# Mask products behind the other sequence's exponent scores, and spline chunks two at a time

## The chip, the cores and the metric

The kernel runs on one core of one Trainium2 chip. The metric is device time in microseconds (us); lower is better. Its five engines each work through their own list of instructions in order and meet at semaphores: TensorE (PE) multiplies, VectorE (DVE) and ScalarE (ACT) empty its results out of PSUM, GpSimd (POOL) does leftovers, and SyncE (SP) issues the DMA transfers.

## The reference

A transformer layer on 16 sequences of 256 tokens, width 256, in float32:

```
x = x + attention(layernorm(x))      # 16 heads of 16; key j counts for query i only if j - i <= 16
x = x + ffn(layernorm(x))            # silu(x @ gate.T) * (x @ up.T) @ down.T, inner width 1024
```

The three weights of the second half are not given as matrices. Each is a cubic (Catmull-Rom) spline through some 2,030 control points, sampled at 262,144 places. The kernel builds them once, at its start.

## The kernel before

The sequences are taken two at a time in eight turns. What a turn does is cut into named steps, and the function `all_steps` (line 109) puts the steps of all turns into one list, sorted by a planned time for each; every engine walks this one list and does its own part of each step. So the table in `steps_of_turn` (line 95) sets the order on every engine, and a turn's attention lies among the second half of the turn before.

The steps that matter here, for each of two sequences (0 and 1) and eight pairs of heads (p), so n = 0 to 15:

- `s1` n: scores of two heads for the row maxima. PE does four products on 63 rows of the array, two in its upper half and two in its lower (line 616), and then two products over all 128 rows that add the mask (line 619): an identity times a triangle of -1e30, in bfloat16. DVE then takes the maxima, two reductions (line 510).
- `mt` s: the 16 heads' maxima of one sequence are turned over and stored by DMA as a 64th row beside the queries (`QM`).
- `sc` n: scores again, transposed, with the maxima taken off by that 64th row. PE does four products on 64 rows (line 636), ACT takes exp (line 418), and POOL cuts away what the mask forbids (lines 366 and 369).
- `av` n: values weighted, for four heads, on column quarters of the array (128*32 in the profile, line 644).
- `zt`, `ot`, `on`, `z2`: transposes. `qk`, `v`, `wo`: projections. `ga`, `up`, `ic`, `dn`: the second half; `ga` and `up` are six products of 512 columns each (lines 566 to 568), `dn`, `v` and `wo` twelve of 256 columns (lines 573 to 575). `x`, `xr`, `ld`, `y`: transfers. `la`, `lb`, `ma`, `mb`: layer norms.
- `ws` u: chunk u of 12 of the spline weights. PE makes two sums over 32 rows (line 589, four records in the trace), DVE joins them in two operations (lines 472 and 474), ACT and POOL split the result in two parts. Chunks 0 to 3 are gate, 4 to 7 up, 8 to 11 down.

`s1`, `sc` and `ws` share two buffers of two PSUM banks each (`pair0`, `pair1`), given in turns in the order of the list; a step on PE first waits until the step before it in its buffer has been emptied (`emptied`, line 244): for `s1` that is DVE's maxima, for `sc` ACT's exp, for `ws` DVE's sum. The other steps share four banks (`ring`). SP waits at each `ld` until `sc` of the turn before no longer reads what is overwritten.

Of the kernel before, what the change touches and what calls it, by code (L numbers as in the profile page):

```python
# [88 lines left out]

PERIOD = 62.0


def steps_of_turn():

    table = [("x", 0, 1, -70.2, 0), ("la", 0, 2, -62.2, 3.4), ("lb", 0, 2, -57.5, 2.25),
# [9 lines left out]
    return [(what, n + i, at + gap * i) for what, n, count, at, gap in table for i in range(count)]  # L107


def all_steps():  # L110

    out = [(t * PERIOD + at, what, t, n) for t in range(TURNS) for what, n, at in steps_of_turn()]
    out += [(-70, "raw", 0, 0), (-51, "split", 0, 0), (-47, "tap", 0, 0)]
    out += [((-33, -30.5, -28)[u] if u < 3 else -27 + 6.5 * (u - 2), "ws", 0, u) for u in range(CHUNKS)]
    return [i[1:] for i in sorted(out, key=lambda i: i[0])]


# [45 lines left out]
def build(nc, x, wqk, wv, wo, points, powers, rows, over, ident, identb, upper, out):  # L163
    ctx = ExitStack()
    with ctx:
# [78 lines left out]
        def emptied(step):  # L244
            what, t, n = step
            if what == "dn":
                return y_done, nth("y", t, n // 4)
            done = {"zt": zt_low, "qk": qk_low, "v": v_done, "mt": mt_done, "av": av_done, "ot": ot_done, "on": on_low,
                    "wo": wo_done, "z2": z2_low, "ga": ga_done, "up": up_done, "s1": max_done, "sc": exp_done,
                    "ws": ws_sum}[what]  # L250
            return done, nth(*step)

# [12 lines left out]
        def raw(i, n):  # L265
            return RAW[:, i * KB * D:(i + n) * KB * D].rearrange("p (k c) -> p k c", k=KB)

        def spline_part(u, part):
            m, j = divmod(u, 4)
            if m < 2:  # L270
                return (WGUh, WGUl)[part][:, m, j // 2, j % 2 * 512:(j % 2 + 1) * 512]
            return WD[:, 2 * j:2 * j + 2, part * D:(part + 1) * D]

        def spline_over(u):
            m, j = divmod(u, 4)
# [174 lines left out]
        def _(dve):  # L450
# [7 lines left out]
            for what, t, n in STEPS:  # L458
# [41 lines left out]
                elif what == "qk":  # L500
                    dve.wait_ge(qk_high, nth("qk", t, n))
                    low(STAGED[n][:, 1, :], bank(what, t, n)[:], STAGED[n][:, 0, :]).then_inc(qk_low, 1)
                elif what == "s1":
                    s, p = divmod(n, NP)
                    dve.wait_ge(s1_made, nth("s1", t, n))
                    if p == 0:
                        if t:
                            dve.wait_ge(mt_made, nth("mt", t - 1, s))
                    for it, cols in ((0, slice(0, W0)), (1, slice(W0, W0 + S))):
                        i = nc.vector.tensor_reduce(out=M[:, s, it, :].rearrange("p (a k) -> p a k", a=2)[:, :, p],  # L510
                                                    in_=pair(what, t, n)[:, :, cols], axis=AX.X, op=ALU.max, negate=True)
                    i.then_inc(max_done, 1)
                elif what == "mt":
                    dve.wait_ge(mt_made, nth("mt", t, n))
                    if t + n:
                        dve.wait_ge(m_loaded[1 - n], N_M * (t + n))
                    nc.vector.tensor_copy(MT[:], bank(what, t, n)[0:H, 0:S]).then_inc(mt_done, 1)
                elif what == "ot":
                    dve.wait_ge(ot_made, nth("ot", t, n))
                    if t:  # L520
                        dve.wait_ge(z2_made, nth("z2", t - 1, n // 2))
                    heads = bank(what, t, n)[:].rearrange("p (h c) -> p h c", c=2 * DH)
                    nc.vector.reciprocal(R[:, n, :], heads[:, :, DH]).then_inc(recip_done, 1)
                    dve.wait_ge(recip_done, nth("ot", t, n))
                    tt(Z[:, n, :].rearrange("p (h c) -> p h c", c=DH), heads[:, :, 0:DH],
                       R[:, n, :].unsqueeze(2).broadcast_to([128, H, DH]), ALU.mult).then_inc(ot_done, 1)
                elif what == "on":
                    dve.wait_ge(on_high, nth("on", t, n))
                    low(OTT[:, 1, :, :], halves(bank(what, t, n)), OTT[:, 0, :, :]).then_inc(on_low, 1)
                elif what == "wo":  # L530
                    dve.wait_ge(xr_loaded[t % 2][n], DMA * (t // 2 + 1))
                    dve.wait_ge(wo_made, nth("wo", t, n))
                    x1 = X1[t % 2][:, 2 * n:2 * n + 2, :]
                    tt(x1, x1, halves(bank(what, t, n)), ALU.add).then_inc(wo_done, 1)
                elif what == "z2":
                    dve.wait_ge(z2_high, nth("z2", t, n))
                    low(seq(YT, 1, n), halves(bank(what, t, n)), seq(YT, 0, n)).then_inc(z2_low, 1)
                elif what == "ga":
                    gu = GU[:, n % 2, :]
                    dve.wait_ge(tanh_done, nth("ga", t, n))  # L540
                    stt(out=gu, in0=gu, scalar=1.0, in1=bank(what, t, n)[:], op0=ALU.add, op1=ALU.mult).then_inc(ga_done, 1)  # L541
                elif what == "up":
                    gu = GU[:, n % 2, :]
                    dve.wait_ge(up_made, nth("up", t, n))
                    dve.wait_ge(ga_done, nth("ga", t, n))
                    tt(gu, gu, bank(what, t, n)[:], ALU.mult).then_inc(up_done, 1)  # L546
                elif what == "y":
                    dve.wait_ge(dn_made, nth("dn", t, 4 * n + 3))
                    x1 = X1[t % 2][:, 2 * n:2 * n + 2, :]
                    tt(x1, x1, halves(bank("dn", t, 4 * n)), ALU.add).then_inc(y_done, 1)  # L550

        @block.tensor
        def _(pe):
# [24 lines left out]
            for what, t, n in STEPS:  # L578
# [3 lines left out]
                    bk = bank(what, t, n)  # L582
                if what == "raw":
                    pe.wait_ge(ident_loaded, DMA)
                elif what == "ws":
                    pe.wait_ge(tapped, 1)
                    m, j = divmod(n, 4)
                    for part in range(2):
                        i = mm(pair(what, t, n)[:, part, :], ROWS[32 * m:32 * m + 32, part, :],  # L589
                               TAP[32 * m:32 * m + 32, j * 512:(j + 1) * 512], start=True, stop=True)  # L590
                    i.then_inc(ws_made, 1)
                elif what == "zt":
                    pe.wait_ge(norm_done[0], nth("lb", t, n))
                    turn_rows(bk, X, n, zt_made)
# [11 lines left out]
                elif what == "s1":  # L606
                    s, p = divmod(n, NP)
                    if p % HP == 0:
                        pe.wait_ge(qk_loaded[s][p // HP], N_QK * (t + 1))
                    if n == 0 and t == 0:  # L610
                        pe.wait_ge(mask_loaded, 2 * DMA)
                    pr = pair(what, t, n)
                    for it, c, w in ((0, 0, W0), (1, W0, S)):
                        for a in range(2):
                            r = slice(STACK * a, STACK * a + STACK - 1)
                            mm(pr[:, a, c:c + w], QM[r, s, p, it * 128:(it + 1) * 128], KS[r, s, p, 0:w],  # L616
                               start=it == 0, stop=False, skip_group_check=True)
                    for a in range(2):
                        i = mm(pr[:, a, AHEAD:AHEAD + 384].rearrange("p (i j) -> p i j", j=128)[:, 0:3:2, :],  # L619
                               IDB[:], UP[:].rearrange("p (i j) -> p i j", i=2), start=False, stop=True,  # L620
                               skip_group_check=True)
                    i.then_inc(s1_made, 1)
                elif what == "mt":
                    pe.wait_ge(max_done, nth("s1", t, n * NP + NP - 1))
# [97 lines left out]
```

## Time and profile before

| what | us |
|---|---|
| three runs, median (lowest to highest) | 720.44 (718.12 to 721.96) |
| profiled execution | 714.97 |
| its span, first to last instruction | 713.2 |
| PE busy in the span | 672.5 (94%) |
| DVE, ACT, POOL busy | 411.2, 263.6, 201.8 |
| mean granted clock of PE | 0.959 of full speed |

PE's matmuls are pipelined: the profile gives each a duration of its own that overlaps the next, so its cost is better read as the distance from its start to the next one's start. A row such as `L616 ... x4` merges neighbouring matmuls of one line. The granted clock has two levels, 1.00 (2.4 GHz) and 0.50 (1.2 GHz). Turns 2 to 6 look alike: from 163 us on, six stretches of 78 us follow each other and the first five differ by nothing that can be seen.

### The profile page before, as it was taken

What the parts mean: (1) busy time and instruction counts of PE and PEld (TensorE: products, weight loads), DVE (VectorE), ACT (ScalarE), POOL (GpSimd) and SP (SyncE); (2) the same over time, 40 slices, a digit from 0 to 9 for tenths busy, and PEclk for the clock granted to TensorE, in tenths of its full rate; (3) what the DMA queues carried; (4) which work ended last, traced back from release to release, by engine and by line L of the source; (5) the groups of instructions that cost most, each with busy time, mean ns of one, the idle gap of its engine ahead of it and who ended that gap; (6) DMA issues with size and microseconds to landing.
All of it is one profiled execution on the core that took longest, in us unless ns stands there. A gap on an engine that the chain in (4) does not pass through costs nothing.

```text
span 713.2 us, 12397 instructions
## 1 busy us (share of the span) xinstructions
PE 672.5 (94%) x4816; PEld 493.4 (69%) x4816; DVE 411.2 (58%) x828; ACT 263.6 (37%) x448; POOL 201.8 (28%) x244
## 2 busy tenths in 40 slices
PE   1799898999999999999999999999999999998997
PEld 0434554677687777877687768777787768776877
DVE  6556566665746475656656574657575563652540
ACT  1212333544433443443433444343433443343140
POOL 5023223213421333114321342124311341243040
PEclk9956697999999999999999999999999999999999
DMA  8221023112212221031201221131202111000000
GB/s 250 91 72 46 1 89 105 47 46 74 74 46 68 83 74 47 16 106 47 88 30 60 76 74 47 42 108 50 72 16 83 53 52 55 21 26 1 31 0 30
DMA packets 42873, 42.75 MB, mean 60 GB/s; under 512 B 4256, under 2 KB 42240, under 8 KB 42496
## 3 DMA queue, kind: packets, MB, share of 16 engines
q1 hardware_dynamic: 42816, 41.96, 17.7%
q8 instruction: 39, 0.64, 0.4%
q14 instruction: 18, 0.15, 0.1%
HBM read 12.32 MB, written 4.19 MB: 23 GB/s over the span
## 4 chain that ended last, share of the span: by engine, by line
PE 89%; DVE 5%; ACT 2%; issue 1%; POOL 1%; DMA 1%; POOLq 0%; ACTq 0%; DVEq 0%
PE ring L566 12%; PE ring L567 10%; PE ring L568 10%; PE ring L644 8%; PE ring L573 8%; PE pair L616 7%; PE ring L574 6%; PE ring L575 6%; PE pair L636 6%; PE pair L619 5%; PE pair L589 4%; PE ring L560 3%; PE ring L651 2%; ACT P L418 2%; DVE X L495 1%
## 5 line engine op out<-in xcount | busy, mean ns | idle before, releaser
L418 ACT ACTIVATE P<-pair 128x800 f32<-128x800 f32 x128 | 107.0, 838 | 133.0 <-PE pair L636 131.6
L510 DVE TENSOR_REDUCE M<-pair 128x2 f32<-128x288 f32 (+1 forms) x256 | 134.7, 569 | 25.8 <-PE pair L619 24.0
L374 POOL TENSOR_TENSOR IN<-GU,IN 128x512 fp32r<-128x512 f32 x64 | 82.3, 1286 | 145.5 <-ACT IN L379 145.5
L366 POOL TENSOR_SCALAR_AFFINE_SELECT P<-P 128x448 f32<-128x448 f32 x64 | 37.3, 582 | 250.3 <-ACT P L418 250.3
L566 PE MATMUL ring<-YT,WGUh 128*128 128x512 f32 x256 | 107.9, 421 | 0.1
L568 PE MATMUL ring<-YT,WGUl 128*128 128x512 f32 x256 | 101.6, 397 | 0.0
L567 PE MATMUL ring<-YT,WGUh 128*128 128x512 f32 x256 | 101.5, 396 | 0.0
L442 ACT ACTIVATE GU<-ring 128x512 f32<-128x512 f32 x64 | 38.3, 598 | 134.0 <-PE ring L568 134.0
L541 DVE SCALAR_TENSOR_TENSOR GU<-GU,ring 128x512 f32<-128x512 f32 x64 | 44.0, 688 | 72.8 <-ACT GU L442 72.8
L573 PE MATMUL ring<-WD,IN 128*128 128x256 f32 x256 | 77.9, 304 | 2.9 <-POOL IN L374 2.9
L616 PE MATMUL pair<-KS,QM 63*128 63x144 f32 (+1 forms) x512 | 67.4, 344 | 7.9 <-DVE M L510 3.2
L575 PE MATMUL ring<-WD,IN 128*128 128x256 f32 x256 | 73.5, 287 | 0.0
L574 PE MATMUL ring<-WD,IN 128*128 128x256 f32 x256 | 73.3, 286 | 0.0
L616 PEld LDWEIGHTS pair<-KS,QM 63*128 63x128 f32 x512 | 41.3, 200 | 43.2 <-issue 27.1
L644 PE MATMUL ring<-P,V 128*32 128x256 f32 (+1 forms) x1024 | 59.6, 352 | 3.3 <-POOL P L369 2.9
L636 PE MATMUL pair<-QM,KS 64*128 64x256 f32 (+1 forms) x512 | 58.4, 309 | 1.1 <-ACT P L418 0.9
L636 PEld LDWEIGHTS pair<-QM,KS 64*128 64x128 f32 x512 | 38.8, 189 | 29.0 <-issue 12.6
L566 PEld LDWEIGHTS ring<-YT,WGUh 128*128 128x128 f32 x256 | 48.2, 188 | 12.3 <-issue 0.5
L546 DVE TENSOR_TENSOR GU<-GU,ring 128x512 f32<-128x512 f32 x64 | 43.8, 685 | 21.8 <-PE ring L568 20.4
L568 PEld LDWEIGHTS ring<-YT,WGUl 128*128 128x128 f32 x256 | 48.2, 188 | 11.3
L567 PEld LDWEIGHTS ring<-YT,WGUh 128*128 128x128 f32 x256 | 48.5, 190 | 8.5
L573 PEld LDWEIGHTS ring<-WD,IN 128*128 128x128 f32 x256 | 49.5, 193 | 6.2 <-issue 4.9
(80 smaller groups left out, 1061.2 us busy)
## 6 DMA issues: line engine op xcount, KB each, us to landing
KS<-QKS SPq DMA_DIRECT2D x96, 128.0 KB, 2.1
QM<-X SPq DMA_DIRECT2D x48, 128.0 KB, 2.1
QM<-QKS SPq DMA_DIRECT2D x48, 128.0 KB, 2.1
X<-x SPq DMA_DIRECT2D x8, 512.0 KB, 3.9
X<-x SPq DMA_DIRECT2D x16, 256.0 KB, 2.9
out<-X SPq DMA_DIRECT2D x16, 256.0 KB, 2.2
OVER<-over SPq DMA_DIRECT2D x1, 1024.0 KB, 12.1
TAP<-points SPq DMA_DIRECT2D x1, 768.0 KB, 7.5
```

The source lines that it names most:

```text
L374: nc.gpsimd.tensor_tensor(IN[:, n, 1, :], GU[:, n % 2, :], IN[:, n, 0, :].bitcast(F32), ALU.subtract).then_inc(in_low, 1)
L418: nc.scalar.activation(P[:, g % 2, 2 * (n % 2):2 * (n % 2) + 2, :], pair(what, t, n)[:, :, 0:SW], ACT.Exp, scale=SCALE).then_inc(exp_done, 1)
L510: i = nc.vector.tensor_reduce(out=M[:, s, it, :].rearrange("p (a k) -> p a k", a=2)[:, :, p], in_=pair(what, t, n)[:, :, cols], axis=AX.X, ...
L566: mm(b[:], wh[:, kb], act[:, 0, kb, :], start=kb == 0, stop=False)
L567: mm(b[:], wh[:, kb], act[:, 1, kb, :], start=False, stop=False)
L568: i = mm(b[:], wl[:, kb], act[:, 0, kb, :], start=False, stop=kb == KB - 1)
L573: mm(b, act(k, 0), w[:, k, 0:D], start=first and k == 0, stop=False, skip_group_check=True)
L574: mm(b, act(k, 0), w[:, k, D:2 * D], start=False, stop=False, skip_group_check=True)
L575: i = mm(b, act(k, 1), w[:, k, 0:D], start=False, stop=False, skip_group_check=True)
L616: mm(pr[:, a, c:c + w], QM[r, s, p, it * 128:(it + 1) * 128], KS[r, s, p, 0:w], start=it == 0, stop=False, skip_group_check=True)
L636: i = mm(pr[:, a, c:c + w], KS[r, s, p, jt * 128:(jt + 1) * 128], QM[r, s, p, S - w:S], start=jt == 0, stop=jt == 1, skip_group_check=True)
L644: i = mm(bk[32 * hl:32 * hl + 32, S - w:S], V[:, n // NG * 2 + jt, n % NG * 4 + hl, :, :].rearrange("p a c -> p (a c)"), P[:, n % 2, hl, c ...
```

## The change

1. **Mask split off.** The two mask products of `s1` become a step `mk` of their own, and DVE's maxima wait for that step. `s1` keeps the four 63-row products.
2. **Beats.** A new table puts `s1` n, `sc` of the other sequence and `mk` n next to each other, sixteen times in a turn: `s1` 0 to 7 of the next turn with `sc` 8 to 15, and `s1` 8 to 15 with `sc` 0 to 7. The other steps are spread anew in between. As the two kinds alternate strictly, every `s1` now takes the same one of the two PSUM buffers and every `sc` the other.
3. **Couples.** Chunks are numbered so that 2k is a gate and 2k+1 an up chunk (rows 0 to 31 and 32 to 63 of the array), and for u below 8 PE does two chunks in one step, their matmuls alternating. Both PSUM buffers must be empty first. Chunks 8 to 11 stay single. `tap`, the operation that prepares their input, stands behind `qk` 2 on DVE, and six chunks stand ahead of the first `s1`.

```diff
+PERIOD = 65.96
+                  ("qk", 0, 4, 1, -59.74, 2.32), ("s1", 0, 8, 1, -31.77, 3.0),
+                  ("mk", 0, 8, 1, -31.73, 3.0), ("ld", 2, 2, 1, -26.2, 11.38),
...
+        def chunk(u):
+            return (u % 2, u // 2) if u < 8 else (2, u - 8)
...
-                elif what == "ws":
+                elif what == "ws" and (n % 2 or n >= 8):
                     pe.wait_ge(tapped, 1)
-                    m, j = divmod(n, 4)
+                    us = (n - 1, n) if n < 8 else (n,)
+                    if n < 8 and BEFORE.get((what, t, n - 1)):
+                        pe.wait_ge(*emptied(BEFORE[what, t, n - 1]))
                     for part in range(2):
-                        i = mm(pair(what, t, n)[:, part, :], ROWS[32 * m:32 * m + 32, part, :],
-                               TAP[32 * m:32 * m + 32, j * 512:(j + 1) * 512], start=True, stop=True)
-                    i.then_inc(ws_made, 1)
+                        for u in us:
+                            m, j = chunk(u)
+                            i = mm(pair(what, t, u)[:, part, :], ROWS[32 * m:32 * m + 32, part, :],
+                                   TAP[32 * m:32 * m + 32, j * 512:(j + 1) * 512], start=True, stop=True)
+                            if part:
+                                i.then_inc(ws_made, 1)
...
                 elif what == "s1":
...
                             mm(pr[:, a, c:c + w], QM[r, s, p, it * 128:(it + 1) * 128], KS[r, s, p, 0:w],
                                start=it == 0, stop=False, skip_group_check=True)
+                elif what == "mk":
+                    if n == 0 and t == 0:
+                        pe.wait_ge(mask_loaded, 2 * DMA)
+                    pr = pair("s1", t, n)
                     for a in range(2):
                         i = mm(pr[:, a, AHEAD:AHEAD + 384].rearrange("p (i j) -> p i j", j=128)[:, 0:3:2, :],
                                IDB[:], UP[:].rearrange("p (i j) -> p i j", i=2), start=False, stop=True,
                                skip_group_check=True)
                     i.then_inc(s1_made, 1)
```

PE in a turn of the middle, before: `sc` 6 (line 636), a step `qk`, and `s1` 14 with its mask (lines 616 and 619).

```order
L636 MATMUL pair0<-QM,KS 128x256 x2
L636 MATMUL pair0<-QM,KS 128x144 x2
L566 MATMUL ring0<-ZT,WQKh 128x512
L567 MATMUL ring0<-ZT,WQKh 128x512
L568 MATMUL ring0<-ZT,WQKl 128x512
L566 MATMUL ring0<-ZT,WQKh 128x512
L567 MATMUL ring0<-ZT,WQKh 128x512
L568 MATMUL ring0<-ZT,WQKl 128x512
L616 MATMUL pair1<-KS,QM 128x144 x2
L616 MATMUL pair1<-KS,QM 128x256 x2
L619 MATMUL pair1<-UP,IDB 128x2x128 x2
```

After, at the same place: a beat of `s1` 14 (L637), `sc` 6 (L661) and `mk` 14 (L644), and the step `up` 0 behind it.

```order
L637 MATMUL pair0<-KS,QM 128x144 x2
L637 MATMUL pair0<-KS,QM 128x256 x2
L661 MATMUL pair1<-QM,KS 128x256 x2
L661 MATMUL pair1<-QM,KS 128x144 x2
L644 MATMUL pair0<-UP,IDB 128x2x128 x2
L584 MATMUL ring0<-YT,WGUh 128x512
L585 MATMUL ring0<-YT,WGUh 128x512
L586 MATMUL ring0<-YT,WGUl 128x512
```

The 63- and 64-row products stand together now, and the full-array mask products moved behind both.

After, on PE: beats 4 and 5 of a turn (counted by the n of `s1`, from 0), with only one `av` (L669) between them, and the first `dn` (L591 to L593) behind.

```order
L637 MATMUL pair0<-KS,QM 128x144 x2
L637 MATMUL pair0<-KS,QM 128x256 x2
L661 MATMUL pair1<-QM,KS 128x256 x2
L661 MATMUL pair1<-QM,KS 128x144 x2
L644 MATMUL pair0<-UP,IDB 128x2x128 x2
L669 MATMUL ring1<-P,V 32x256 x4
L669 MATMUL ring1<-P,V 32x144 x4
L637 MATMUL pair0<-KS,QM 128x144 x2
L637 MATMUL pair0<-KS,QM 128x256 x2
L661 MATMUL pair1<-QM,KS 128x256 x2
L661 MATMUL pair1<-QM,KS 128x144 x2
L644 MATMUL pair0<-UP,IDB 128x2x128 x2
```

The second `s1` goes to the same `pair0` as the first, which DVE must have read by then.

At the start, after, PE has the chunks in couples (L611), the two buffers alternating; before it had two matmuls of one buffer, then two of the other.

```order
L611 MATMUL pair0<-TAP,ROWS 128x512
L611 MATMUL pair1<-TAP,ROWS 128x512
L611 MATMUL pair0<-TAP,ROWS 128x512
L611 MATMUL pair1<-TAP,ROWS 128x512
L611 MATMUL pair0<-TAP,ROWS 128x512
L611 MATMUL pair1<-TAP,ROWS 128x512
```

Six such rows are one and a half couples; three couples now come ahead of the first `s1`, where three single chunks came before.

## Rows read from the trace of the kernel before

**Rows 1.** The page: the chain that ended last, share of the span by engine.

```profile
PE 89%; DVE 5%; ACT 2%; issue 1%; POOL 1%; DMA 1%; POOLq 0%; ACTq 0%; DVEq 0%
```

**Rows 2.** Windows: from:to, length, busy us (count) per engine, clock, DMA share, GB/s.

```profile
30.00:115.00 85.00, 79.36 (x380) 40.96 (x379) 51.10 (x92) 23.28 (x41) 22.37 (x24) 0.74 0.19 63
...
163.00:241.00 78.00, 77.60 (x600) 58.83 (x601) 47.35 (x100) 31.70 (x55) 22.26 (x28) 1.00 0.19 62
...
631.00:713.00 82.00, 73.35 (x474) 61.63 (x472) 30.24 (x54) 22.42 (x39) 22.78 (x24) 0.96 0.04 14
```

**Rows 3.** Timeline of PE, turn 4: start, us, line, operation, tiles, shape, count.

```profile
330.49 0.50 PE L616 MATMUL pair<-KS,QM 63*128 63x144 f32 x4
330.92 0.39 PE L619 MATMUL pair<-UP,IDB 128*128 128x256 bf16 x2
331.07 0.47 PE L566 MATMUL ring<-YT,WGUh 128*128 128x512 f32 x1
331.38 0.40 PE L567 MATMUL ring<-YT,WGUh 128*128 128x512 f32 x1
331.62 0.40 PE L568 MATMUL ring<-YT,WGUl 128*128 128x512 f32 x1
...
335.31 0.28 PE L574 MATMUL ring<-WO,OTT 128*128 128x256 f32 x1
335.43 0.28 PE L575 MATMUL ring<-WO,OTT 128*128 128x256 f32 x1
335.64 0.45 PE L636 MATMUL pair<-QM,KS 64*128 64x256 f32 x4
336.02 0.50 PE L566 MATMUL ring<-YT,WGUh 128*128 128x512 f32 x1
336.36 0.40 PE L567 MATMUL ring<-YT,WGUh 128*128 128x512 f32 x1
```

**Rows 4.** Timeline of PE where `s1` directly follows `sc`, and the next.

```profile
346.88 0.45 PE L636 MATMUL pair<-QM,KS 64*128 64x256 f32 x4
347.17 0.43 PE L616 MATMUL pair<-KS,QM 63*128 63x144 f32 x4
347.54 0.39 PE L619 MATMUL pair<-UP,IDB 128*128 128x256 bf16 x2
348.26 0.50 PE L616 MATMUL pair<-KS,QM 63*128 63x144 f32 x4 [0.33 <-ACT P L418]
```

**Rows 5.** Timeline of DVE, ACT and POOL in the same stretch.

```profile
347.96 2.21 DVE L510 TENSOR_REDUCE M<-pair 128x2 f32<-128x288 f32 x4 [0.29 <-PE pair L619]
347.37 0.84 ACT L418 ACTIVATE P<-pair 128x800 f32<-128x800 f32 x1 [2.13 <-PE pair L636]
348.11 0.62 ACT L379 ACTIVATE IN<-GU 128x512 fp32r<-128x512 f32 x1
349.42 1.27 POOL L374 TENSOR_TENSOR IN<-GU,IN 128x512 fp32r<-128x512 f32 x1
```

**Rows 6.** Timeline of PE at the start.

```profile
30.14 6.49 PE L589 MATMUL pair<-TAP,ROWS 32*128 32x512 f32 x12
...
40.67 3.78 PE L589 MATMUL pair<-TAP,ROWS 32*128 32x512 f32 x4
...
65.36 0.69 PE L636 MATMUL pair<-QM,KS 64*128 64x256 f32 x8
...
106.75 0.50 PE L616 MATMUL pair<-KS,QM 63*128 63x144 f32 x4 [0.50 <-DVE W L474]
```

**Rows 7.** Timeline of DVE at the start.

```profile
21.50 2.28 DVE L466 TENSOR_TENSOR TAP<-TAP,POWER 96x2048 f32<-96x2048 f32 x1
...
44.49 0.69 DVE L472 TENSOR_TENSOR W<-pair,OVER 128x512 f32<-128x512 f32 x1 [2.65 <-PE pair L589]
```

**Rows 8.** Timeline of PE in the last turn.

```profile
650.90 0.89 PE L644 MATMUL ring<-P,V 128*32 128x256 f32 x16 [2.03 <-POOL P L369]
...
668.87 0.63 PE L560 MATMUL ring<-ID,Z 128*128 128x128 f32 x4 [0.46 <-DVE Z L495]
```

More of the change, by code:

```diff
@@ L87, in spline_tables, with steps, steps_of_start @@
             over.astype(np.float32))
-PERIOD = 62.0
-def steps_of_turn():
-    table = [("x", 0, 1, -70.2, 0), ("la", 0, 2, -62.2, 3.4), ("lb", 0, 2, -57.5, 2.25),
[9 rows of a table removed]
-    return [(what, n + i, at + gap * i) for what, n, count, at, gap in table for i in range(count)]
+PERIOD = 65.96
+def steps(table):
+    return [(what, n + by * i, at + gap * i) for what, n, count, by, at, gap in table for i in range(count)]
+def steps_of_start():
+    return steps([("raw", 0, 1, 1, -100.24, 0), ("split", 0, 1, 1, -63.32, 0), ("tap", 0, 1, 1, -54.24, 0),
+                  ("ws", 0, 4, 2, -45.21, 6.09), ("ws", 1, 4, 2, -45.18, 6.09),
+                  ("ws", 8, 4, 1, 24.16, 6.37)])
+def steps_of_turn():
+    return steps([("x", 0, 1, 1, -90.73, 0), ("la", 0, 2, 1, -73.48, 2.94), ("lb", 0, 2, 1, -69.39, 2.04),
[14 rows of a table added]
 def all_steps():
-    out = [(t * PERIOD + at, what, t, n) for t in range(TURNS) for what, n, at in steps_of_turn()]
-    out += [(-70, "raw", 0, 0), (-51, "split", 0, 0), (-47, "tap", 0, 0)]
-    out += [((-33, -30.5, -28)[u] if u < 3 else -27 + 6.5 * (u - 2), "ws", 0, u) for u in range(CHUNKS)]
+    out = [(at, what, 0, n) for what, n, at in steps_of_start()]
+    out += [(t * PERIOD + at, what, t, n) for t in range(TURNS) for what, n, at in steps_of_turn()]
     return [i[1:] for i in sorted(out, key=lambda i: i[0])]
@@ L247, in emptied @@
                 return y_done, nth("y", t, n // 4)
+            if what == "s1":
+                return max_done, nth("mk", t, n)
             done = {"zt": zt_low, "qk": qk_low, "v": v_done, "mt": mt_done, "av": av_done, "ot": ot_done, "on": on_low,
-                    "wo": wo_done, "z2": z2_low, "ga": ga_done, "up": up_done, "s1": max_done, "sc": exp_done,
+                    "wo": wo_done, "z2": z2_low, "ga": ga_done, "up": up_done, "sc": exp_done,
                     "ws": ws_sum}[what]
@@ L274, in spline_over @@
         def spline_over(u):
-            m, j = divmod(u, 4)
+            m, j = chunk(u)
             if m < 2:
@@ L502, in _ @@
                     low(STAGED[n][:, 1, :], bank(what, t, n)[:], STAGED[n][:, 0, :]).then_inc(qk_low, 1)
-                elif what == "s1":
+                elif what == "mk":
                     s, p = divmod(n, NP)
-                    dve.wait_ge(s1_made, nth("s1", t, n))
+                    dve.wait_ge(s1_made, nth("mk", t, n))
                     if p == 0:
@@ L510, in _ @@
                         i = nc.vector.tensor_reduce(out=M[:, s, it, :].rearrange("p (a k) -> p a k", a=2)[:, :, p],
-                                                    in_=pair(what, t, n)[:, :, cols], axis=AX.X, op=ALU.max, negate=True)
+                                                    in_=pair("s1", t, n)[:, :, cols], axis=AX.X, op=ALU.max, negate=True)
                     i.then_inc(max_done, 1)
@@ L584, in _ @@
                     pe.wait_ge(ident_loaded, DMA)
[L585 removed]
+                elif what == "ws" and (n % 2 or n >= 8):
                     pe.wait_ge(tapped, 1)
[L587 removed]
+                    us = (n - 1, n) if n < 8 else (n,)
+                    if n < 8 and BEFORE.get((what, t, n - 1)):
+                        pe.wait_ge(*emptied(BEFORE[what, t, n - 1]))
                     for part in range(2):
[L589 to L591 removed]
+                        for u in us:
+                            m, j = chunk(u)
+                            i = mm(pair(what, t, u)[:, part, :], ROWS[32 * m:32 * m + 32, part, :],
+                                   TAP[32 * m:32 * m + 32, j * 512:(j + 1) * 512], start=True, stop=True)
+                            if part:
+                                i.then_inc(ws_made, 1)
                 elif what == "zt":
@@ L617, in _ @@
                                start=it == 0, stop=False, skip_group_check=True)
+                elif what == "mk":
+                    if n == 0 and t == 0:
+                        pe.wait_ge(mask_loaded, 2 * DMA)
+                    pr = pair("s1", t, n)
                     for a in range(2):
@@ L623, in _ @@
                 elif what == "mt":
[L624 removed]
+                    pe.wait_ge(max_done, nth("mk", t, n * NP + NP - 1))
                     for it in range(2):
```

3 lines of the change are left out of this document (removed), and 21 rows, old and new, of tables (PERIOD, table).

## The prediction

> **What bounds the kernel now.** I read the chain of waits first: 89% of the span is PE's own work [rows 1]. Then the windows by stage [rows 2]. In a middle turn PE is busy for 77.60 of 78.00 us at full clock, so there a turn gets shorter only if PE's own list gets shorter. From 30 to 115 us PE is busy for 79 of 85 us, but at a mean clock of 0.74; the half clock lasts from about 34 to 62 us and comes back in pieces. In the last 82 us PE waits for some 9. Third I read PE's timeline for what stands between matmuls [rows 3, 4], since a busy share of 99% hides what a matmul costs beyond its columns.
>
> **What a change of shape costs.** The array is used in three shapes: all 128 rows (F), halves of 63 or 64 rows (R: `s1`, `sc`), column quarters (C: `av`). In F, six-matmul steps go start to start in 0.24 us (331.38 to 331.62) and 256-column ones in 0.12 (335.31 to 335.43). Around R it is more. The last F matmul before `sc` takes 0.21, 0.09 over its 0.12. `sc` takes 0.38 to the next F step (335.64 to 336.02), but 0.29 where `s1` follows (346.88 to 347.17): 0.09 for leaving R. The first F matmul behind takes 0.34 (336.02 to 336.36), 0.10 over. And `s1` takes 0.43 to its mask when it comes from F (330.49 to 330.92), 0.37 when it comes from `sc` (347.17 to 347.54): 0.06 for entering. An excursion F-R-F thus costs 0.09 + 0.06 + 0.09 + 0.10 = 0.34 us beyond its columns [rows 3, 4].
>
> **Beats, in a middle turn.** Before, a turn has 16 excursions for `s1` and 16 for `sc`, less the two places where `s1` comes directly behind `sc` (behind `sc` 13 and `sc` 4). After, each of 16 beats is one excursion, with `mk` as its way back into F. Fourteen excursions go. If `s1` to `sc` is as free as `sc` to `s1` is in rows 4, each is worth 0.32 to 0.34: 14 x 0.33 = 4.6 us. The trace has no `s1` followed directly by `sc`. From below: if there the array had to empty as well, each beat gives back 0.09 + 0.06 and more of the entry, and about 0.15 stays, 14 x 0.15 = 2.1 us. From above: no stall anywhere else, 4.8. I take 0.30 a beat, near the seamless row since both kinds use the same halves: 4.2 us. No column is saved; the mask products only move.
>
> **The waits that beats bring.** `s1` n+1 now needs the buffer of `s1` n, so a beat cannot be shorter than a loop: `s1` and `sc` together about 0.56 (0.43 + 0.29, less the exits), `mk` start to maxima start 0.42 (347.54 to 347.96), maxima 1.10 (half of 2.21), and 0.05 to PE (exp ends at 347.37 + 0.84 = 348.21, PE goes at 348.26): 2.13 us [rows 4, 5]. For `sc` it is 0.49 + 0.84 + 0.05 = 1.4, never the later. PE's own work in a beat is about 0.83 for the three steps plus what stands between. Going through the sixteen gaps of a turn: 15 hold at least one six-matmul step, 12-matmul step or more (0.83 + 1.4 = 2.2 or more, just over the loop), one holds only `av` 5: 0.83 + 0.82 = 1.65, a stall of 0.5. In the gap behind beat 1 (one `ga`) 0.1 is to spare. What else is in DVE's list ahead of the maxima must be counted too: in beat 4 the product of `up` 7 (0.69, as other operations of that size, rows 7) ends before the mask does; behind beat 1 a layer norm and `ga` 6 delay the next maxima by about 0.4, where PE has 3.1 us of work; behind beat 8 five operations of 0.7 make 3.5 us, where PE has 3.8 to the next beat and that one's maxima are wanted 4 us later. `dn` 0 needs `ic` 7: 0.8 + 0.62 + 1.27 + hops = 2.9 us after `up` 7 [rows 5], and PE arrives at 2.13 + 0.83 = 2.96. All hidden, some by a tenth. Old stalls that go: 0.33 behind `sc` 13 [rows 4]. New 0.5 less old 0.33: +0.2, and 0.1 for near misses. Turn: 78.0 - 4.2 + 0.3 = 74.1 us. If the near misses all miss (0.3 us in six gaps) it is 75.7. Five middle turns: 5 x 3.9 = 19.5 us.
>
> SP's list: before, the two transfers of the maxima's row (`mt` 0) stood ahead of the six of `ld` 3, now behind. `sc` 15 releases `ld` 3, whose issues take some 3.8 us, then the two of `mt`, 1.4, and about 2 to land: 7.7 us behind `sc` 15, where PE has 9.6 us of work before `sc` 0 needs them. Hidden by 2 us. The two `ld` for `qk` stand earlier in SP's list than before and hold back one store and one load of `xr`, which nothing wants for 14 us.
>
> **The start.** Taken one by one. (a) `tap` (2.28 us, rows 7) ran on DVE while `qk` 0 was on PE; behind `qk` 2 it holds back the first chunk: 30.1 becomes 32.5, +2.3. (b) A single chunk takes PE 3.8 us at half clock (the row at 40.67) [rows 6], so about 1.9 at full. Chunks of a couple lie in different quarters of rows. The trace has no matmuls in two such quarters; `av`'s four column quarters and the two halves of `sc` do overlap. If they overlap fully a couple costs what one chunk did; if not at all, double. I take the first. But a couple fills both buffers and the next waits until DVE has emptied both, 4 x 0.7 = 2.8 us [rows 7], so three couples take 32.5 to about 51 (2 + 2.8, then twice 3.7 + 2.8, starts overlapping ends a little), and the fourth, behind two `s1`, ends on DVE at 60. With `s1` 2 to 7 at 1.27 each, `mt` and two `v`, `sc` 0 comes at 73 where it was at 65.4 [rows 6]: +8. (c) From there to `s1` 0 of turn 1 it was 41.4 us (65.36 to 106.75), with five chunks and `sc` 8, 9. Now two chunks, no `sc` 8, 9: at full clock 8 beats of 1.0 (with both shape changes to F), `zt`, `qk`, `av`, two chunks 3.8, transposes, 23 us; with the loop of 2.13 in the empty gaps 24.5; with part of it at half clock, as before, 28. That is -13. (d) The first half of turn 1 has the loop in nearly every gap and two chunks: I take it as even, between -2 and +2. (e) Its second half, an estimate from half of a middle turn's gain, is -2. Sum: +8 - 13 - 2 = -7, between -14 (full clock early) and +6 (couples that do not overlap: the first one 1.9 more, three 3.7: 13).
>
> The Trainium skill, TensorEngine Tiling (Array Packing), section PSUM Bottleneck, speaks against the couples: tiling speeds up TensorE and not the emptying of PSUM, which may become the bound. Here the trace bears it out in DVE's 2.8 us a couple against 1.9 on PE at full clock; by it the couples bring nothing ahead of the first `s1`, as step (b) has it from rows.
>
> **The end.** The last turn has beats too: -2 for its first half, -1.4 for its second (empty gaps at the loop's 2.1). Behind it, `av` 6, which waited 2.03 us for POOL, has a `dn` ahead now and waits no longer, -2.4 with what hangs on it; but `z2` 1, which waited 0.46 us for the layer norm with two `dn` to cover it, has one `dn` less (1.4), and `ga` 0 behind it has no `dn` to hide `z2`'s copy and subtraction (0.6 + 0.69 + hops): +2.8 [rows 8]. Together -3.
>
> **Sum.** 713.2 - 19.5 - 7 - 3 = 683.7 us of span; the execution adds 1.8 (714.97 to 713.2), and the median of the runs stands 1.008 times over the profiled one (720.44 to 714.97): 691 us.
>
> **Rivals.** *Couples do not overlap*, or DVE cannot keep up with them at half clock: step (b) costs 13 more. For: no row shows two 32-row quarters at once. Against: `av`. 691 + 13 = 704. *The maxima bound the beats*: 2.13 us in more gaps than one, since each `s1` now has one buffer where two were open; 1.9 us a turn more, 7.5 turns, 14 us: 705. For: 0.1 us of slack at `dn` 0 and behind beat 1. Against: DVE is busy for only 47 of 78 us. *A shape change is paid at s1 to sc as well*: 2.1 instead of 4.2 a turn, 7.5 turns, 16 us: 707. Against: rows 4, in the other direction. *The clock falls in the beats*, the other side: in the first eight beats PE would wait a little in each gap and run small shapes, and the granted clock, which is 1.00 in all middle turns and 0.50 from 34 to 62 us, when chunks and `s1` alternated, would fall there too. 10 us at half clock cost 5 us a turn, more than beats save; at 10 us in each of seven turns, and the start no better, 720 + 7 = 727. It turns the sign at 8 us a turn. Against: six of eight gaps hold F work, and in the old turn three `s1` and two `sc` nearly side by side left it at 1.00.
>
> The Trainium skill, TensorE: Matmul & The Clock Gate, section "A second HAM failure mode: psum-queue depth-cycling", describes that very fall when PE pauses briefly between groups for its PSUM buffers; the middle turns here show none, with a pause of 0.33 us among them.
>
> **Numbers.** Forecast 0.60; couples 0.14; maxima 0.11; shape change 0.08; clock 0.04; 0.03 for no change by several small ones. The forecast's own range is 682 to 700. Forecast 691; range 676 to 708, which holds the three middle rivals and leaves out some 0.15. A measurement tells 0.5% (3.6 us) from nothing: faster 0.93, same 0.03, slower 0.04.
>
> **What would show it.** A turn's period of 74 us, PE busy in nearly all of it at clock 1.00. `s1` to `sc` 0.27 to 0.3, `sc` to `mk` 0.27 to 0.38. One stall of 0.5 us per turn, between beats 4 and 5, put down to the maxima. A couple of chunks at 1.9 or 3.7 us, not double. First `sc` at 73, `s1` of turn 1 near 101. Wrong: a period of 76 or more, stalls on maxima in many gaps, or a clock below 1.00 in a middle turn.

## The result

| | before | after |
|---|---|---|
| median of the runs, us | 719.28 (716.72 to 721.96) | 696.66 (692.05 to 697.20) |
| ratio, 95% interval | | 0.967 (0.962 to 0.973) |
| span of the profiled execution | 713.2 | 695.0 |
| its mean granted clock | 0.959 | 0.934 |

The change makes the kernel faster by 3.3%. The median is 6 us slower than the forecast of 691 and inside its range. The medians differ by 22.6 us, the profiled executions by 18.2; the reason is taken up with e5_oldstart below. The 18.2 us are the sum of three stretches, read from the starts of `s1` 0: turn 2 begins 12.1 us **later** (183.5 instead of 171.4), the five middle turns take 362.3 instead of 390.0, 27.8 less, and from turn 7 to the end it is 2.5 less. The windows of after answer to [rows 2].

```profile
30.00:72.00 42.00, 28.70 (x105) 14.35 (x105) 25.20 (x48) 6.30 (x11) 11.61 (x10) 0.55 0.23 77
72.00:106.00 34.00, 29.32 (x202) 17.09 (x200) 17.97 (x33) 13.38 (x22) 7.22 (x10) 0.80 0.19 63
106.00:146.00 40.00, 32.69 (x200) 19.39 (x200) 18.39 (x43) 11.26 (x19) 9.35 (x13) 0.57 0.17 54
...
328.00:401.00 73.00, 72.66 (x603) 58.06 (x603) 46.84 (x102) 32.39 (x55) 22.57 (x28) 1.00 0.20 66
```

A middle turn is still all PE (72.66 of 73) at full clock. The start is not: from 106 to 146 us, the first half of turn 1, the mean clock is 0.57 and PE is idle for 7 us. Up to `s1` 0 of turn 2 the clock was at 0.50 for 85 us, where the trace of before has 51.

Two beats of a middle turn, PE's timeline of after, to be held against [rows 3, 4]:

```profile
342.82 0.50 PE L637 MATMUL pair<-KS,QM 63*128 63x144 f32 x4
343.15 0.35 PE L661 MATMUL pair<-QM,KS 64*128 64x256 f32 x4
343.44 0.39 PE L644 MATMUL pair<-UP,IDB 128*128 128x256 bf16 x2
343.76 0.88 PE L669 MATMUL ring<-P,V 128*32 128x256 f32 x16
344.98 0.50 PE L637 MATMUL pair<-KS,QM 63*128 63x144 f32 x4 [0.34 <-DVE M L528]
345.32 0.35 PE L661 MATMUL pair<-QM,KS 64*128 64x256 f32 x4
345.60 0.39 PE L644 MATMUL pair<-UP,IDB 128*128 128x256 bf16 x2
```

`s1` takes 0.33 to `sc`, that 0.29 to `mk`, and `mk` 0.15 where a six-matmul step follows (0.20 to 0.32 at five of the sixteen): 0.77 us as a rule, where before the isolated steps took 0.58 and 0.38. The one wait of the turn is the forecast one, between beats 4 and 5, for DVE's maxima: 344.98 - 342.82 = 2.16 us of loop (2.13 forecast). The idle time shown is 0.34; `av` 5 takes 1.22 us to the next start, where 0.81 is usual, so 0.41 is lost.

The weight loads (PEld) of the same beat show what stands at a change of shape:

```profile
343.04 0.31 PEld L661 LDWEIGHTS pair<-QM,KS 64*128 64x128 f32 x4
343.44 0.11 PEld L644 LDWEIGHTS pair<-UP,IDB 128*128 128x128 bf16 x2
```

Between `s1` and `sc` the load starts 0.12 us ahead of its matmul (343.15), while `s1` still runs. At `mk`, where the shape changes, load and matmul start together (343.44). This holds for all such borders in turns 2 to 6: between full-array and 63- or 64-row products (264 borders before, 129 after) the load is never more than 5 ns ahead, between steps of the full array it is 25 to 239 ns ahead, and between `s1` and `sc` 116 to 123 ns. So at a change of shape nothing of the load is hidden behind the matmul before it. Whether the array must also run empty can't be seen in these rows.

By kind of step, start to start over turn 4 (so each step also carries what it costs to reach the next one's shape):

| us in a turn | before | after |
|---|---|---|
| `s1` with mask | 10.79 | 8.20 |
| `sc` | 6.10 | 4.51 |
| `av` (with the stall behind it) | 6.52 | 6.92 |
| all others | 54.60 | 52.80 |
| sum | 78.01 | 72.43 |

The table agrees with the count of shape changes: PE enters the 63- and 64-row shape 30 times in this turn before and 16 times after. The others do the same matmuls in 1.8 us less; they border on another shape less often.

### The profile page after: what moved, and what is told of

It reads as the page before. It is cut to its first block, busy times and chain, and to the rows that moved or that the text cites. A ratio compares the mean times of both kernels' runs of the same rounds, so it can differ in the third digit from the quotient of the medians.

```text
span 695.0 us, 12397 instructions
## 1 busy us (share of the span) xinstructions
PE 635.3 (91%) x4816; PEld 486.6 (70%) x4816; DVE 403.8 (58%) x828; ACT 270.6 (39%) x448; POOL 203.9 (29%) x244
## 4 chain that ended last, share of the span: by engine, by line
PE 88%; DVE 8%; issue 1%; ACT 1%; DMA 1%; POOL 1%; POOLq 0%; DVEq 0%
PE ring L584 11%; PE ring L586 11%; PE ring L585 11%; PE pair L637 8%; PE ring L591 7%; PE ring L669 7%; PE ring L592 7%; PE ring L593 7%; PE pair L644 6%; PE pair L611 4%; PE pair L661 4%; PE ring L578 3%; DVE M L528 3%; PE ring L676 2%; DVE X L513 1%; DVE W L490 1%
## 5 line engine op out<-in xcount | busy, mean ns | idle before, releaser
L591 PE MATMUL ring<-WD,IN 128*128 128x256 f32 x256 | 76.9, 300 | 4.2 <-POOL IN L392 4.2
L637 PE MATMUL pair<-KS,QM 63*128 63x144 f32 (+1 forms) x512 | 68.2, 347 | 10.1 <-DVE M L528 7.1
L637 PEld LDWEIGHTS pair<-KS,QM 63*128 63x128 f32 x512 | 41.2, 199 | 47.5 <-issue 21.2
L593 PE MATMUL ring<-WD,IN 128*128 128x256 f32 x256 | 72.9, 285 | 0.0
L592 PE MATMUL ring<-WD,IN 128*128 128x256 f32 x256 | 72.7, 284 | 0.0
L397 ACT ACTIVATE IN<-GU 128x512 fp32r<-128x512 f32 x64 | 40.2, 629 | 70.3 <-DVE GU L564 70.2
L669 PE MATMUL ring<-P,V 128*32 128x256 f32 (+1 forms) x1024 | 60.0, 354 | 0.0
L584 PEld LDWEIGHTS ring<-YT,WGUh 128*128 128x128 f32 x256 | 48.5, 189 | 12.7 <-issue 3.3
L564 DVE TENSOR_TENSOR GU<-GU,ring 128x512 f32<-128x512 f32 x64 | 44.0, 688 | 18.1 <-PE ring L586 14.2
L644 PE MATMUL pair<-UP,IDB 128*128 128x256 bf16 x256 | 53.7, 294 | 0.0
L591 PEld LDWEIGHTS ring<-WD,IN 128*128 128x128 f32 x256 | 49.0, 191 | 6.0 <-issue 3.5
## 6 DMA issues: line engine op xcount, KB each, us to landing
OVER<-over SPq DMA_DIRECT2D x1, 1024.0 KB, 12.2
```

What stands on the lines that cost most here:

```text
L584: mm(b[:], wh[:, kb], act[:, 0, kb, :], start=kb == 0, stop=False)
L591: mm(b, act(k, 0), w[:, k, 0:D], start=first and k == 0, stop=False, skip_group_check=True)
L592: mm(b, act(k, 0), w[:, k, D:2 * D], start=False, stop=False, skip_group_check=True)
L593: i = mm(b, act(k, 1), w[:, k, 0:D], start=False, stop=False, skip_group_check=True)
L669: i = mm(bk[32 * hl:32 * hl + 32, S - w:S], V[:, n // NG * 2 + jt, n % NG * 4 + hl, :, :].rearrange("p a c -> p (a c)"), P[:, n % 2, hl, c ...
```

## The experiments

Each changes the changed kernel unless it says otherwise.

**One part undone: the mask directly behind `s1` (e3_swap).**

```diff
-                  ("mk", 0, 8, 1, -31.73, 3.0), ("ld", 2, 2, 1, -26.2, 11.38),
+                  ("mk", 0, 8, 1, -31.745, 3.0), ("ld", 2, 2, 1, -26.2, 11.38),
...
-                  ("s1", 8, 8, 1, -2.08, 3.0), ("sc", 0, 8, 1, -2.06, 3.0),
+                  ("s1", 8, 8, 1, -2.08, 3.0), ("sc", 0, 8, 1, -2.03, 3.0),
...
-                  ("on", 0, 2, 1, 33.45, 33.19), ("sc", 8, 8, 1, 34.22, 3.0),
+                  ("on", 0, 2, 1, 33.45, 33.19), ("sc", 8, 8, 1, 34.23, 3.0),
```

> The changed kernel with one thing undone: in every beat the mask products stand directly behind s1 again and sc comes last (s1, mk, sc). Same beats, same gaps, same buffers. Theory shape: a beat then has two excursions from the full array instead of one: by the rows of before 0.43 + 0.32 + 0.38 = 1.13 us instead of 0.77 for the three steps, and 0.1 more behind them or less; 16 x 0.36 = 5.8 us a turn, less the 0.4 stall that goes: turn 72.4 to about 77.8, time 697 + 7.5 x 5.4 = 737, slower than before the change. Rival: the gain of a turn is owed to the new spread of the other steps and fewer waits: under 702.

The time is 732.87 us (731.99 to 733.99), 1.019 (1.016 to 1.023) of before, so slower than the kernel before the change. PE's timeline at the same beat:

```profile
357.93 0.50 PE L637 MATMUL pair<-KS,QM 63*128 63x144 f32 x4
358.36 0.39 PE L644 MATMUL pair<-UP,IDB 128*128 128x256 bf16 x2
358.68 0.45 PE L661 MATMUL pair<-QM,KS 64*128 64x256 f32 x4
359.06 0.88 PE L669 MATMUL ring<-P,V 128*32 128x256 f32 x16
```

0.43 + 0.32 + 0.38 = 1.13 us, where after has 0.94 at the same place (342.82 to 343.76) and 0.77 to 0.85 elsewhere. Turns take 77.9 (from 264.06 to 575.70 for four), and `s1` with mask and `sc` account for 5.4 us of the 5.5. PE waits nowhere in these turns, so the stall of 0.41 is gone too: 5.9 us for 16 more visits to the small shape, 0.37 each. The mask is in bfloat16 and its neighbours are not, but PE goes into bfloat16 and out of it once a beat in either order, so that isn't what differs.

Nearly all of the 5.6 us that a middle turn had gained is gone with the order inside the beats. The turn has two visits more than before (32 for 30) and is as long; by the price above the new spread of the other steps can be worth half a microsecond at most. The Trainium skill, TensorEngine Tiling (Array Packing), Key Properties, says that changing the mode empties TensorE. The pair of timelines agrees that each change costs time; that the time is an emptying no run shows.

**Couples undone, numbering kept (e2_single).**

```diff
-elif what == "ws" and (n % 2 or n >= 8):
+elif what == "ws":
...
-    us = (n - 1, n) if n < 8 else (n,)
-    if n < 8 and BEFORE.get((what, t, n - 1)):
-        pe.wait_ge(*emptied(BEFORE[what, t, n - 1]))
+    us = (n,)
```

> The changed kernel with couples undone on PE: the same list and numbering, each chunk a step of its own that waits for its own buffer. Theory overlap: the two 32-row products of a couple run at the same time, a couple takes 1.9 or 3.7 us like one chunk; without couples six chunks ahead of the first s1 take 6 x 3.7 = 22 us instead of 17, and chunks 6 and 7 one more 3.7: 697 + 6 to 9 = 703 to 706. Rival: emptying on DVE (2.8 us a couple) is the bound and couples bring nothing: 697.

The time is 691.63 us (688.70 to 692.99), ratio 0.961 (0.957 to 0.965). Neither theory holds: it is 5 us faster than the changed kernel. PE's chunks in after, then in e2_single:

```profile
37.19 3.78 PE L611 MATMUL pair<-TAP,ROWS 32*128 32x512 f32 x8 [2.87 <-DVE W L492]
43.81 3.78 PE L611 MATMUL pair<-TAP,ROWS 32*128 32x512 f32 x8 [2.84 <-DVE W L492]
49.07 0.80 PE L637 MATMUL pair<-KS,QM 63*128 63x144 f32 x4 [1.47 <-DVE W L492]
```

```profile
35.82 5.10 PE L609 MATMUL pair<-TAP,ROWS 32*128 32x512 f32 x8 [1.48 <-DVE W L492]
41.10 5.10 PE L609 MATMUL pair<-TAP,ROWS 32*128 32x512 f32 x8 [0.18 <-DVE W L492]
46.38 0.80 PE L635 MATMUL pair<-KS,QM 63*128 63x144 f32 x4 [0.18 <-DVE W L492]
```

A couple does take 3.78 us at half clock, as one chunk did [rows 6]: the quarters overlap. But PE then waits 2.8 us until DVE has emptied both buffers. As single steps, two chunks take 5.10 us, also less than twice 3.78, because neighbours still lie in different quarters, and the next one starts when its own buffer is free. So I had undone the wait and not the overlap.

**Numbering undone too (e11_serial).**

```diff
-            return (u % 2, u // 2) if u < 8 else (2, u - 8)
+            return divmod(u, 4)
```

> As e2_single (single chunks, the changed list), but numbered as before: 0 to 3 gate, 4 to 7 up, so that neighbouring chunks are in the same quarter of rows but for 3 and 4. Theory overlap: in e2_single neighbours in different quarters run at the same time although each is a step of its own (chunk 3 starts 2.3 us behind chunk 2 at half clock, where one alone takes 3.7); without that the six chunks ahead of s1 0 take 6 x 3.7 = 22 us less the first at full clock, s1 0 comes at 52 instead of 46.4, chunks 6 and 7 add 2 more: 691.6 + 7 = 699. Rival: DVE's 1.4 us a chunk and the buffers set the pace: no change, 692.

The time is 695.09 us (693.84 to 696.77). `s1` 0 comes at 49.81 (46.38 in e2_single, 49.07 in after). Chunks 1 and 2, in one quarter, start 3.41 us apart, and so do 2 and 3; chunks 3 and 4, the one pair of neighbours in two quarters, start 2.56 us apart (clock 0.50). So the overlap hangs on the quarters. It is worth 3.4 us up to `s1` 0 and 3.5 us of the time, where theory overlap had 5.6 and 7: DVE and the buffers set part of the pace. The couples with their double wait are 0.7 us ahead of the serial chunks at this point, which is nothing that a timed run can tell.

**Couples alone, on the kernel before (e4_couples).** Its own table, with chunks 0 to 7 in couples at four places:

```diff
-((-33, -30.5, -28)[u] if u < 3 else -27 + 6.5 * (u - 2), "ws", 0, u)
+((-33, -28, -17, -4)[u // 2] + u % 2 * 0.001 if u < 8 else -27 + 6.5 * (u - 2), "ws", 0, u)
```

> The kernel before with the couples alone: its own table of steps, with chunks 0 to 7 numbered and multiplied in couples that stand at four places (two couples ahead of the first s1, one behind s1 3, one behind mt 0). No beats. Theory overlap: four PE steps of 1.9 to 3.7 us go, 719 - 10 = 709, turns of 78.0. Rival: nothing, 719, since each couple must wait for both buffers and DVE.

The time is 714.50 us (711.54 to 718.73, ten runs), ratio 0.993 (0.990 to 0.995), 5.6 less than before. Its profiled execution was its slowest (718.73), and that of before (714.97) was faster than all its timed runs, so their traces can't be set against each other for this. The chunks' places, their numbering and the couples were all changed together here, so the 5.6 us can't be given to the couples alone; it is less than the 10 expected.

**Chunks 8 to 11 out of turn 1 (e6_chunks).**

```diff
-("ws", 8, 4, 1, 24.16, 6.37)
+("ws", 8, 4, 1, 7.2, 6.1)
```

> The changed kernel with chunks 8 to 11 moved out of the first half of turn 1 (behind beats 11, 13 and 15 of turn 0 and behind mt 1). Theory buffers: two of them hold score buffers in turn 1, PE waits 1.5 us behind each and spends 3.7 on each at half clock, so the stretch from s1 0 to s1 8 of turn 1 falls from 39.6 to about 31, while the stretch ahead of it grows by 4: time 697 - 5 = 692. Rival clock alone: the beats wait for maxima anyway at half clock, the stretch falls by the two chunks' own 5.6 and the stretch ahead grows by as much: 697.

The time is 692.35 us (690.76 to 692.81), ratio 0.960 (0.954 to 0.966). The stretch from `s1` 0 to `s1` 8 of turn 1 falls from 39.6 to 27.4 us, that from `s1` 8 of turn 0 to `s1` 0 of turn 1 grows from 33.8 to 42.6. The total of 4.3 us is near theory buffers' 5, but both stretches moved more than it said (12.2 for 8.6, 8.7 for 4), and the clock moved as well: in the first stretch it was at 0.50 for 14.0 us, in after for 33.8. How much came from the buffers and how much from the clock is not told apart. In after the two chunks do this:

```profile
110.03 1.98 PE L611 MATMUL pair<-TAP,ROWS 32*128 32x512 f32 x4
111.94 0.50 PE L637 MATMUL pair<-KS,QM 63*128 63x144 f32 x4
113.91 0.70 PE L661 MATMUL pair<-QM,KS 64*128 64x256 f32 x4 [1.47 <-DVE W L492]
114.55 0.61 PE L644 MATMUL pair<-UP,IDB 128*128 128x256 bf16 x2
116.31 0.80 PE L637 MATMUL pair<-KS,QM 63*128 63x144 f32 x4 [1.15 <-DVE M L528]
...
122.22 3.77 PE L611 MATMUL pair<-TAP,ROWS 32*128 32x512 f32 x4 [1.15 <-DVE M L528]
125.92 0.80 PE L637 MATMUL pair<-KS,QM 63*128 63x144 f32 x4
127.88 0.70 PE L661 MATMUL pair<-QM,KS 64*128 64x256 f32 x4 [1.16 <-DVE W L492]
```

A chunk takes one of two score buffers, so `sc` stands behind it until DVE has done the chunk, `mk` stands behind `sc`, and the maxima behind `mk`.

**Fewer maxima in turn 1 (e7_halfmax).** One of two reductions left out in turn 1, sequence 0.

```diff
-for it, cols in ((0, slice(0, W0)), (1, slice(W0, W0 + S))):
+for it, cols in ((0, slice(0, W0)), (1, slice(W0, W0 + S)))[:1 if t == 1 and s == 0 else 2]:
```

> The changed kernel with one of the two maxima reductions of each of eight beats left out (turn 1, sequence 0): the loop from s1 to the next s1 is shorter by 0.53 us there, nothing else changes. Theory loop: in those beats PE waits for maxima, so each gets 0.5 us shorter where nothing else stands between (behind beats 1, 4, 6, with av or nothing) and, if the shorter wait brings the clock back, more: -2 to -8 us, 689 to 695. Rival: the waits there are not what the time goes by, PE's own half-clock work is: 697.

The time is 694.38 us (693.16 to 694.57), and the stretch is 36.2 instead of 39.6 us, inside what theory loop had. The loop through DVE is a bound of those beats. Part of the gain is the clock's, which theory loop had left open: it was at 0.50 for 24.6 us of the stretch instead of 33.8.

**Useless work in the same beats (e1_fill).**

```diff
+FILLED, FILL = ((1, 0),), 3
...
+                if what == "s1" and (t, n // NP) in FILLED:
+                    other = ("sc", t, n - NP) if n >= NP else ("sc", t - 1, n + NP)
+                    pe.wait_ge(*emptied(BEFORE[other]))
+                    for _ in range(FILL):
+                        mm(pair(*other)[:, 0, :], WQKh[:, 0, 0:128], WQKh[:, 0, :], start=True, stop=True)
```

> The changed kernel with useless work added: in the first half of turn 1, ahead of each of the eight beats, PE does three full-array matmuls of 512 columns into the other score buffer once that is free (their result is overwritten). Theory clock: beats without second-half work leave PE waiting for maxima, the granted clock is 0.50 from 113 to 143 us, and that is why the stretch from s1 0 to s1 8 of turn 1 takes 39.6 us instead of 26.9. Then more work keeps the clock at 1.00, the stretch falls to about 30 us and the time from 696.7 to about 688. Rival waits: the buffers' waits themselves cost the time; then 24 added matmuls change nothing or add up to 6 us, 697 to 703.

The time is 699.21 us (698.88 to 702.09). The clock of the stretch rises, and nothing is won:

```profile
105.00:148.00 43.00, 35.53 (x219) 21.34 (x217) 17.85 (x43) 10.81 (x18) 9.41 (x13) 0.73 0.15 50
```

0.73 instead of 0.57, but the stretch takes 42.9 us instead of 39.6: the 24 matmuls take 11 us, of which 7.6 are given back. Changing PE's work moved its clock, here and in e6_chunks and e7_halfmax, each in one traced execution; but theory clock wanted 1.00 and the clock came to 0.73, so what a full clock would bring stays open. Bought with work it costs more than it brings.

**Useless work between the first chunks (e10_startfill),** on e9_best below: four such matmuls into a free ring bank ahead of chunks 0, 2, 4 and 6.

```diff
+if n < 8 and n % 2 == 0:
+    pe.wait_ge(*emptied(BEFORE["mt", 0, 0]))
+    for _ in range(4):
+        mm(bank("mt", 0, 0)[:], WQKh[:, 0, 0:128], WQKh[:, 0, :], start=True, stop=True)
```

> As e9_best, with useless work: ahead of each even chunk of the first eight PE does four full-array matmuls of 512 columns into a free ring bank (overwritten later). Theory clock: the half clock from 34 us on comes from PE streaming through 32 of 128 rows and waiting; full-array work in between (1 us at full clock) holds the clock at 1.00, chunks take 1.9 us instead of 3.7, and s1 7 of turn 0 comes some 4 us sooner in spite of 16 added matmuls: e9_best - 3. Rival: the clock falls all the same and the work is only added: e9_best + 4 to 6.

The time is 688.78 us (685.13 to 690.90), 6.3 more than e9_best. The two windows are its own:

```profile
30.00:40.00 10.00, 7.20 (x29) 3.71 (x28) 6.03 (x9) 2.28 (x5) 3.19 (x3) 1.00 0.53 184
40.00:65.00 25.00, 21.16 (x76) 10.56 (x76) 14.69 (x27) 3.09 (x5) 6.94 (x6) 0.50 0.17 53
```

e9_best has 0.63 and 0.53 in these windows. The clock fell at 40.1 us instead of 32.5, behind the third group of four, and came to 0.50 all the same, as the rival had it.

**The old start ahead of new turns (e5_oldstart).** The list of before up to `s1` 0 of turn 2 (its masks written as `mk` directly behind `s1`), single chunks in alternating quarters, and then the changed list.

```diff
-    return [i[1:] for i in sorted(out, key=lambda i: i[0])]
+    out = [i[1:] for i in sorted(out, key=lambda i: i[0])]
+    start = old_start()
+    return start + [i for i in out if i not in start]
```

> Single chunks as in e2_single, and the list of the kernel before up to s1 0 of turn 2 (s1, mask and sc apart, chunks scattered, tap early), then the changed list with its beats. Theory start: the changed kernel reaches s1 0 of turn 2 at 183.5 us, before at 171.4, and e2_single at 179.9; the 12 us are owed to the order of the start alone, above all to the eight beats of turn 1 without second-half work. Then s1 0 of turn 2 comes near 173 and the time is e2_single's 691.6 - 6 = 685, with turns of 72.4 unchanged. Rival: early beats are good and the time was lost by something else (chunk numbering, couples): 692 or more.

The time is 692.19 us (691.46 to 693.72), no better than e2_single's: theory start missed. Turn 2 starts at 178.6, not at 173. PE did before's list up to there, yet came 7 us later than the trace of before. The windows up to `s1` 0 of turn 1, of before and then of e5_oldstart, differ in the clock:

```profile
30.00:107.00 77.00, 71.92 (x321) 36.17 (x320) 46.04 (x82) 20.33 (x36) 19.98 (x21) 0.73 0.18 63
```

```profile
30.00:112.00 82.00, 76.42 (x316) 38.35 (x312) 44.93 (x79) 20.06 (x35) 19.97 (x21) 0.65 0.16 55
```

The first time at half clock ended at 61.7 us in the one and at 80.9 in the other. So the trace of before seems to show a start luckier than its usual one, though the chunks' numbering differs as well. The timed runs of before bear it out. All 31 beside the experiments, from 715.4 to 724.1 us, were slower than the profiled execution (714.97, mean clock 0.959), and their time goes with their mean clock: 0.954 to 0.955 from 715.4 to 716.9 us, 0.948 around 720, 0.941 to 0.943 from 721.5 up. The profiled execution of after (696.75) is a usual one (median 696.66). Of the 12 us that after's start seemed to lose, some 4 are that: the 22.6 us between the medians less the 18.2 between the traces.

**`av` 4 behind beat 4 (e8_av4).**

```diff
-("av", 4, 4, 1, 41.51, 6.04)
+("av", 4, 1, 1, 47.0, 0), ("av", 5, 3, 1, 47.55, 6.04)
```

> The changed kernel with av 4 moved from behind beat 2 to behind beat 4, so that behind beat 4 two av stand (1.6 us) and PE should not wait for the maxima there. Theory loop: the beat's loop of 2.16 us is covered, the stall of 0.41 us in each turn goes: period 72.44 to 72.05, time 697 - 3 = 694. Rival: exp of sc 12 now waits for av 4, sc 13 for exp 12, and as much is lost one beat later: 697.

The time is 694.74 us (693.07 to 695.86), too near the 696.66 to tell by itself, but the trace does; the period is 72.23 (four turns from 256.14 to 545.07), 0.21 less: half of the stall. The other half is the rival's: exp of `sc` 12 now waits for `av` 4, starts 1.95 us behind its beat's start instead of 1.38, and `sc` 13 and the mask behind it go 0.2 us later.

**Everything that helped (e9_best):** e2_single, e6_chunks, e8_av4 and `tap` at -62.0 instead of -54.24.

> The changed kernel with four repairs together: single chunks in alternating quarters (as e2_single), chunks 8 to 11 moved into turn 0 (as e6_chunks), av 4 behind beat 4 (as e8_av4), and tap ahead of qk 0 on DVE, where before had it. Theory: the parts add, 696.7 - 3.8 - 3.9 - 2.0 and -2 for the first chunk 2 us sooner = 685. Rival: they act on the same idle time at the start, and the later ones bring nothing: 689 to 691.

The time is 682.46 us (678.26 to 684.07, six runs), ratio 0.947 (0.944 to 0.950): 14.2 us less than the changed kernel and the fastest of all. The three parts that ran alone gave 5.0, 4.3 and 1.9 us, 11.2 together, so they add; the earlier `tap`, expected at 2, was not run alone and is left with 3.0. `s1` 0 of turn 0 comes at 43.3, turn 2 at 172.0, and turns take 72.2.

## Why the prediction was right, and where it was not

**Beats: right in kind, 8 us too small.** The mechanism stood, and e3_swap shows it alone. The term was mis-sized: 4.2 us of shape changes a turn, 3.9 with the waits. Measured are 5.7 of shape changes (78.01 less the old stall of 0.33, against 72.43 less the new one of 0.41) and 5.6 in all. By the prediction's prices the borders of the other steps should have given 14 x 0.19 = 2.7 and gave 1.8. The three steps themselves should have given 16 x 0.13 = 2.1 and gave 3.9, and there two things were priced wrong. They take mostly 0.77 and not 0.83. And I took every `s1` before at its isolated 0.58; where its mask stood directly ahead of `sc`, `av` or another `s1`, six times a turn, it took 0.75 or more (`s1` 0 of turn 4: 327.36 to 328.11), since the mask is itself a short stay in the full shape.

**Waits of beats: right.** Loop 2.16 for 2.13, one stall of 0.41 for 0.5, no other. `dn` 0 met its bound by a hair, as worked out: it started at 345.80, with nothing shown as a wait. In the first half of turn 1, at half clock, the rival *maxima* did come true: PE waits 1.15 us for them behind each of beats 1, 3 and 5.

**SP's order: right.** No middle turn has a wait for the maxima's row. The sum had a slip: 3.8 + 1.4 + 2 is 7.2 us and not 7.7.

**Start, steps (a) and (b): right.** The first chunk came at 32.3 us (32.5 forecast) and the first `sc` at 72.7 (73), and the couples overlapped. The price of the couples was seen and its remedy was not: PE waited 2.8 us at each couple for both buffers. The Trainium skill, TensorEngine Tiling (Array Packing), section PSUM Bottleneck, says that emptying PSUM may become the bottleneck once tiling has sped up TensorE. The trace agrees for the couples alone: as single steps the same chunks wait 1.48 us for DVE ahead of the first pair and then 0.18, so the bound was the double wait and not DVE's pace.

**Start, steps (c) to (e): wrong, and this is where 19 us went.** The sum said -7 and the trace shows +12: (c) -7.9 for -13, (d) +12.7 for "even", (e) 0 for -2. In (c) both chunks (8 and 9) fell in half clock, from 92.2 us on, and took 3.71 us each, where 3.8 for the two had been counted; turn 1 began at 106.2 and not near 101. For (d) I counted the loop in the empty gaps at full clock and the two chunks at their own time. Left out was what a chunk does to the beat behind it (e6_chunks), and that the loop is longer at half clock: 0.59 + 0.47 + 0.54 = 1.6 us of PE (116.31 to 117.91) for what is 0.77 at full, then DVE (e7_halfmax). In this stretch PE has little to do and waits often, and the clock was at 0.50 for 33.8 of 39.6 us, where before had 10.2 of 26.9. An estimate from these: 23.6 us more at half clock are worth up to 11.8 of the 12.7, had PE been busy all the time. So the clock is likely the largest thing that the step left out. I had its fall as a rival, but in middle turns, where it did not come, and not in the start, where I had seen it in [rows 2]. Why it stayed down for so long is open. In (e) I took half of a middle turn's gain, but the stretch now also holds `up` 4 and `on` 0 (1.93 us), which before stood behind `s1` 0 of turn 2, for `sc` 8 and 9 (0.76), which have left it. And part of the 12 us is no loss: the trace that I measured from was a lucky one (e5_oldstart).

**End: -2.5 for -3.** `z2` 1 waited 1.89 us for the layer norm (0.46 and 1.4 priced) and `ga` 0 behind it 1.50 us, and `av` 6 waited no longer.

**The final number** is nearer than its terms. The middle turns gained 8.3 us more than forecast and the start lost 19 more, and these two partly cancel: -29.5 was the sum of span and -18.2 came. Scaling by 720.44/714.97 to the median took the traced execution of after to be a lucky one as well, which it was not, and gave 5.5 us back. That is chance, not method.

## What to carry to other kernels

Where PE is full, count its changes of shape, not only its columns: products on a half array next to one another, and full-array work behind both, saved 7% of a turn with not one column less to multiply. When two steps are coupled so that they overlap, couple only the order and not their waits. And price a start by what its few independent steps make each engine wait for, with a second execution at hand, since the clock there varies from run to run (mean clock 0.941 to 0.959 for the kernel before).

## What the runs showed of the hardware

At a change between full-array and 63- or 64-row products the weight load starts with its matmul (0 to 5 ns ahead, 264 borders before and 129 after), where it otherwise starts up to 239 ns ahead; each visit to the small shape cost 0.37 us (e3_swap against after). Going from 63 to 64 rows has no such cost (load 116 to 123 ns ahead).

Steps of one instruction list overlap on TensorE across step borders when they lie in different quarters of rows: two chunks of 3.78 us in 5.10 (e2_single), with no coupling in the code. Within one quarter they start 3.41 us apart (e11_serial).

Adding 24 full-array matmuls went with a granted clock of 0.73 instead of 0.57 in a stretch of some 40 us (e1_fill). With twelve such matmuls from 29.5 to 39.7 us the clock first fell at 40.1 us (e10_startfill), where the twelve other traces have the fall between 31.9 and 34.6. What in PE's work decides the clock was not settled: it fell to 0.50 at 34 us both in before, with PE busy for 5.00 of the 5 us from 30 on, on 32-row products for the most part, and in after, with PE busy for 2.11 of them.
